# A perceiver's first loop on one core: three moves in TensorE's order, one in ScalarE's

## The reference

```python
h = layernorm(x); Q = h @ wq; K = ctx @ wk; V = ctx @ wv          # layer 0 cross-attention
x = x + softmax(Q @ K.T) @ V
h = layernorm(x)                                                  # layer 0 mixer
gate = sigmoid(h @ W_gate.T + b_gate)
xp, dp = split(h @ W_in.T + b_in); delta = relu(dp)
# for each of 512 channels and 16 states: s_t = s_(t-1) * exp(A * delta_t) + xp_t * delta_t * B
x_mid = x + (gate * (s @ c0 + xp * D_vec)) @ W_out.T + b_out
k = focused(ctx @ Wk + bk); v = ctx @ Wv + bv                     # layer 1 cross-attention, context side
kv = einsum('bhjc,bhjd->bhcd', k, v);  ksum = k.sum(rows)
```

## Time and profile before

| what | value |
|---|---|
| median of 3 runs | 2238.33 us |
| range of the runs | 2237.59 to 2258.23 us |
| profiled execution | 2234.23 us, span 2232.4 us |
| TensorE busy over the span | 1853.6 us (83%) |
| VectorE, ScalarE, GpSimd busy | 1592.1, 1477.1, 1209.7 us |
| mean granted TensorE clock | 0.928 |

### The profile page before, as it was taken

The page is one execution under the profiler, slowest core; times in us unless marked ns, Lnnn a source line. Parts: engine busy times, 40 slices in busy tenths (PEclk is TensorE's granted clock), DMA queues, the critical chain, the costliest instruction groups (busy, mean ns, idle before and its releaser), DMA issues. The chain is left out here.

```text
span 2232.4 us, 41590 instructions
## 1 busy us (share of the span) xinstructions
PE 1853.6 (83%) x14324; PEld 1242.3 (56%) x14355; DVE 1592.1 (71%) x2945; ACT 1477.1 (66%) x3431; POOL 1209.7 (54%) x1300
## 2 busy tenths in 40 slices
PE   4899889989989899899899865368888888988874
PEld 2665555555555555565565422256666666666752
DVE  3348777767867867868678686457888878788763
ACT  2558877878868868878778766124656666666654
POOL 1435655545546555545545533156777777677751
PEclk9999999999999999999999986679989999899875
DMA  7322122212221111212121110100000000000000
GB/s 179 121 74 76 44 69 70 62 55 67 68 71 59 63 62 60 64 57 79 43 69 41 38 47 5 54 7 9 13 12 12 12 12 12 12 12 12 10 9 10
DMA packets 48370, 103.20 MB, mean 46 GB/s; under 512 B 6384, under 2 KB 25072, under 8 KB 43376
## 3 DMA queue, kind: packets, MB, share of 16 engines
q1 hardware_dynamic: 48240, 101.57, 14.4%
HBM read 93.03 MB, written 8.52 MB: 45 GB/s over the span
## 5 line engine op out<-in xcount | busy, mean ns | idle before, releaser
L861 POOL TENSOR_TENSOR kcube<-kcube,ksq 128x512 f32<-128x512 f32 x128 | 178.3, 1393 | 474.2 <-ACT ksq L718 474.2
L696 ACT ACTIVATE abuf<-delta,cols 128x496 f32<-128x496 f32 x512 | 338.5, 699 | 30.5 <-DVE gP L943 14.5
L871 POOL TENSOR_TENSOR yac<-yac,gP 128x1024 f32<-128x1024 f32 x128 | 302.3, 2362 | 11.2 <-ACT gP L705 10.1
L943 DVE TENSOR_TENSOR_SCAN gP<-abuf,ps_s 128x512 f32<-128x512 f32 x256 | 293.3, 1196 | 0.6 <-POOL yac L871 0.6
L524 PE MATMUL ps_kv<-kcube,cx 128*128 128x256 f32 x1024 | 249.3, 387 | 40.3 <-ACT kcube L736 39.4
L943 DVE TENSOR_TENSOR_SCAN gL<-abuf,ps_s 128x512 f32<-128x512 f32 x192 | 223.3, 1207 | 57.3 <-ACT abuf L696 57.1
L512 PE MATMUL ps_kv<-w_k,cT 128*128 128x256 f32 x1024 | 255.6, 392 | 0.0
L524 PEld LDWEIGHTS ps_kv<-kcube,cx 128*128 128x128 f32 x1024 | 191.8, 192 | 100.7 <-ACT kcube L736 63.0
L570 PE MATMUL ps_t<-gL,diag 128*128 128x512 f32 x384 | 192.1, 624 | 54.3 <-DVE gL L943 49.0
L512 PEld LDWEIGHTS ps_kv<-w_k,cT 128*128 128x128 f32 x1024 | 184.4, 190 | 49.3 <-issue 29.4
L583 PE MATMUL ps_kv<-hT,w_pT 128*128 128x512 f32 x384 | 186.9, 610 | 18.8 <-ACT delta L769 14.5
(11 more groups left out here) (312 smaller groups left out, 4253.0 us busy)
## 6 DMA issues: line engine op xcount, KB each, us to landing
cT<-in_h_ctxT SPq DMA_DIRECT2D x32, 1028.0 KB, 4.9
cx<-in_ctx SPq DMA_DIRECT2D x32, 1024.0 KB, 5.5
xT<-in_h_xT SPq DMA_DIRECT2D x8, 512.0 KB, 3.7
xcur<-in_x SPq DMA_DIRECT2D x32, 128.0 KB, 2.0
x_mid<-xb SPq DMA_DIRECT2D x16, 256.0 KB, 2.2
x_c<-x_mid SPq DMA_DIRECT2D x32, 128.0 KB, 2.0
out<-y SPq DMA_DIRECT2D x32, 128.0 KB, 1.7
kv_all<-vleft SPq DMA_DIRECT2D x8, 256.0 KB, 10.5
```

The lines of the kernel that those rows point to most:

```text
L696: act.activation(abuf[q % 2][:, i, :].rearrange("p (b t) -> p b t", t=T)[:, :, 1:T], delta[J % 2][:, :].rearrange("p (b t) -> p b t", t=T) ...
L861: pool.tensor_tensor(t[:, :, :], t[:, :, :], ksq[:, :, :], ALU.mult).then_inc(S["k3_ready"], 1)
L871: pool.tensor_tensor(yac[:, :, :], yac[:, :, :], pool_home(q)[:, :, :], ALU.add).then_inc(S["pacc_done"], 1)
L943: dve.tensor_tensor_scan(dst[:, i, :], abuf[q % 2][:, i, :], ps_u[:, :], 0.0, ALU.mult, ALU.add).then_inc(S["scan_done"], 1)
```

## The change

In TensorE's order, keys 1 move from behind the transposes of the attention weights to ahead of context product 2, in every step with an A. In steps with `g == 3`, the first half of the queries moves ahead of keys 3, while the second stays at the end. Keys 3, context product 0 and L559 then lie between the halves. In steps with `g == 0`, the second half of the output projection moves behind keys 3. Keys 3 then lie between those halves. In ScalarE's order, the copy of the first query half moves ahead of the second squares of keys 2, the copy of context product 0 and the layer norm (L834). No operation, wait, buffer or transfer is added or removed, and the order in which `ps_p` is used stays the same.

```diff
@@ def pe_step
             pe_project(pe, "x", J)
+        if A is not None:
+            pe_keys(pe, A, 1)
         if C is not None:
             pe_gram(pe, C, 2)
...
             pe.transpose(ps_m[:, 2 * P:3 * P], plm[:, :], ident[:, :]).then_inc(S["pT_full"], 1)
-            pe_keys(pe, A, 1)
         if Z is not None:
             pe_states(pe, Z, 7)
...
             last.then_inc(S["o_full"], 1)
+        if g == SG - 1 and sc < NS - 1:
+            pe_queries(pe, sc + 1, 0)
+
+        if A is not None:
+            pe_keys(pe, A, 3)
         if g == 0 and sc >= 2:
             pe_out(pe, sc - 2, 1)
-
-        if A is not None:
-            pe_keys(pe, A, 3)
+        if A is not None:
             pe_gram(pe, A, 0)
         if C is not None:
             pe_sums(pe, C)
-        if g == SG - 1 and sc < NS - 1:
-            pe_queries(pe, sc + 1, 0)
-
         if g == SG - 1 and sc < NS - 1:
             pe_queries(pe, sc + 1, 1)
@@ def act_step
             act_weigh(act, J, 3)
+        if g == SG - 1 and sc < NS - 1:
+            act_query(act, sc + 1, 0)
         if A is not None:
             act_square(act, A, 2, False)
...
                            scale=rstd1[:, 0:1]).then_inc(S["lnh_ready"], 1)
-        if g == SG - 1 and sc < NS - 1:
-            act_query(act, sc + 1, 0)
```

## The result

The changed kernel takes 2228.77 us (median of 20 runs, 2223.46 to 2233.56). The kernel before takes 2239.98 us (20 runs beside them, 2234.32 to 2262.47). The ratio is 0.9944 with a 95% interval of 0.9927 to 0.9960, so the change saves 0.6%, some 11 to 12 us. The forecast was 2220, within 2209 to 2233.

The account below looks back on a forecast made before the run. Bound: a ring of ScalarE, GpSimd and VectorE in ordinary steps, TensorE's order in g = 0 steps and the start. -12.9 - 9.4 - 0.8 - 1.2 + 6.4 = -17.9 us from 2238.3 gives 2220, range 2209 to 2233.

Parts of the forecast that it names:

- part 1: Output halves, six g = 0 steps: keys 3 fill the gap before the second half; 2.15 us each, 12.9 us.
- rival B: The start gains nothing, as the copy of product 2 or GpSimd's powers come last there; 2230 us, chance 10%.
- Part 2: Keys 1 in 21 ordinary steps: gap moves to before product 3, about 1.2 us; gain taken as zero.
- The ring: Ordinary steps: a chain through ScalarE, GpSimd and VectorE, without TensorE, sets the period of 37.45 us.
- Part 3: Keys 1 in steps 0 to 3: fill TensorE's gaps, less slowed clock; 9.4 us saved, between 5 and 10.5.
- part 4: Query halves, steps 3 to 27: scores stay, gap only shifted; gain 0 in six steps, 0.8 us in step 3.
- the gap of 1.25 us: TensorE's gap in step 0, read as having keys 1 behind it; counted as 1.25 us gained.
- The clock: Longer gap before the scores halves TensorE's rate in four of six cases; 6.4 us lost, between 0 and 9.6.
- The rival "the clock doesn't fall": TensorE's clock stays up in front of the scores; 2214 us, chance 14%.
- The credit of 1.2 us for slow second halves: Second query halves: three slow ones, each delaying ScalarE's second copy by 0.4 us, are gone; 1.2 us saved.
- the gap of 3.5 us: TensorE's new idle time before the scores, after the second query half moves earlier; 3.5 us.

Follow-up runs that it names:

- The part runs: Parts of the change against the kernel before: output halves 0.9958, keys 1 0.9982, query halves with ScalarE's first copy 1.0072, keys 1 with output halves 0.9927.

## Why the prediction was right, and where it was off

**Direction and range were right, the size was not.** 17.9 us were forecast and 11.2 came. Of the 8.8 us between 2220 and 2228.8, 1.6 are the median of before, which is 2240.0 over 20 runs where three had given 2238.3. In the records the parts add up to step 31: -14.1 us in the g = 0 steps by part 1, -9.2 up to step 4, +11.3 for the clock and -0.9 in all other steps give the 12.9 us by which step 31 starts earlier. The time by itself doesn't support the forecast: it lies nearer to rival B's 2230 (nothing gained at the start) than to 2220, and the range held it partly because it was drawn wide enough for B. Only the traces tell the two apart, since the start did gain.

**Part 1 was right.** 2.15 us a step were expected, 2.24 to 2.35 measured wherever the clock stayed up, and no cover was lost.

**Part 2 was right.** Ordinary steps didn't move, with 1.29 us of new gap where 1.2 were expected, ended by ScalarE's copy. The ring was named rightly as the bound, by 0.3 us. But step 18 doesn't stand for all 21 of these steps. ScalarE's scalings of pair 1 in steps 17, 18 and 19 start at 674.95, 712.40 and 749.85 us in the kernel before, and the next two 41.3 and 44.4 us apart, so the period of 37.45 us occurs twice in a supergroup. I hadn't looked at how far the next limit lay behind. That margin is what a change to VectorE or GpSimd would have met.

**Part 3 and the start of part 4 were right in the main.** 10.2 us were expected up to step 4, and 9.24 measured, 8.7 of them behind the first scores. Keys 1 alone gave 6.5 of the 9.4 of part 3, and up to 7.4 in the runs that move the output halves too. One reading was wrong: in step 0 keys 1 (at 48.95 us) stood ahead of the gap of 1.25 us, not behind it. From the scores of step 0 to those of step 1 the changed kernel took 18.6 us, and 18.5 before, with the scores of step 0 at the lower clock (1.94 us instead of 1.08). With keys 1 alone it was 16.9.

**The clock was the mis-sized term.** "I take four of the six at 1.6 us, which is 6.4 us lost, between 0 and 9.6." In the records five of six fell and lost 11.3 us, above the upper bound too. This is 4.9 us more than the sum had, and most of its error. The run with three useless matmuls puts the whole term at 9.7 us of the medians, or 8.7 by the two ratios. The number of falls was nearly right; their length was not. I had taken 1.6 us from one row, a stretch of 3.47 us, and three of the five here lasted 6.8 us and cost 2.6 to 2.8 us. The traces of before already had a slowed stretch of that length at step 1, which I used for another term. The rival "the clock doesn't fall" was priced at 2214, and the run that realises it gave 2216.6.

**The credit of 1.2 us for slow second halves is real but doesn't show in the total.** With only the query halves moved, all g = 3 steps took 45.56 us where the mean of before is 45.75, which is 1.1 us in six steps. In the changed kernel they took 45.81. Keys 1 account for this: beside the output halves they lengthen the g = 3 steps from 45.55 to 45.76 us and shorten the g = 1 steps from 34.61 to 34.39.

**Part 4 as a whole.** That the scores would stay was right, and so was the gap of 3.5 us. What I didn't draw from the sum is that the move was worse than nothing: priced by itself it is -0.8 - 1.2 + 6.4 us, and I left that as one term among others. The part runs show some 4 to 5 us lost beside the other two parts, and 16.7 alone. The 12 us between these two values belong to the same edit, with its gaps at other times; why it hurts less beside the other parts I have not isolated.

**What stays open.** Which of the gaps of 2.6 to 2.8 us lower the clock is not explained by their length. From step 31 to the loop's end the records of after are 3.3 us longer than those of before, with about as much time at the lower clock (58 us after, 55 before). Over the fourteen traces this part took 176.4 to 180.1 us, and with the query halves moved alone 178.8, so the 3.3 us may be no part of the change. Open too is the part behind the first loop, which was longer in every kernel with the query halves moved.

## What to carry to other kernels

When a step starts one engine's work earlier, follow the result to the last instruction that releases the consumer. If that one keeps its place in another engine's order, the idle time is only moved together, and one long gap can cost more than two short ones. Move the releasing instruction too: here the edit that lost 4 to 5 us gained some 15 once the second copy moved with it (ratio 0.9860 instead of the 0.9927 of keys 1 and output halves). A clock term should be sized by the longest slowed stretch that the traces show, not by the one row that looks most alike, and a fill of useless matmuls, sized from a measured row, is a cheap way to measure it.

## What the runs showed of the hardware

**The clock's loss depends on more than the gap.** The gap of 2.65 us ahead of the second output half never lowered the clock in the kernel before and did so in three of six steps when only the query halves had moved. The gap ahead of the second query half lowered it in three of six steps at 2.61 us in the kernel before. At 2.83 us it did so in six of six with keys 1 alone, and in one of six with keys 1 and the output halves. A gap of 3.52 us ahead of the scores was followed by the lower level in five of six steps of the changed kernel and in six of six with the query halves alone. From step 4 to step 31 of the fourteen traces a stretch at the lower level lasted from 3 to 10.5 us.

**VectorE beside GpSimd.** With GpSimd's cube beside it, VectorE's third operation of the block's end took 1.63 us (L1015 in the changed kernel, where the cube took 1.76 us). With the addition moved ahead, the two no longer lay beside each other, and the same operation took 0.69 us and the cube 1.27. Not every operation suffers: L1013, which adds two SBUF operands too, lay beside the same cube from 709.98 us on and took 0.69 us. The rows of the changed kernel, VectorE and then GpSimd:

```profile
709.92 0.69 DVE L1013 TENSOR_TENSOR yg<-yg,yac 128x512 f32<-128x512 f32 x1
710.65 1.63 DVE L1015 SCALAR_TENSOR_TENSOR yg<-gate,yg 128x512 f32<-128x512 f32 x1
```

```profile
709.98 1.76 POOL L862 TENSOR_TENSOR kcube<-kcube,ksq 128x512 f32<-128x512 f32 x1 [0.88 <-ACT ksq L719]
```

In L1015 and in the cube both engines read two operands from SBUF. The Trainium skill (GPSIMD Engine Reference, section "8. Key points") says that GpSimd shares its SBUF interfaces with VectorE and contends with VectorE instructions that have two SBUF inputs. The two pairs of durations agree with that, and L1013 shows that it doesn't hold for every such operation.
